# Attention operands stacked by selection matmuls, scores on 32-row tiles two heads at a time, and all experts kept in SBUF, in a two-block transformer kernel on one core

## What is computed

```python
x = x + tanh(g_xattn) * cross_attention(layernorm(x), ctx)       # one head of width 128, 512 keys of width 96
h = rmsnorm(layernorm(x)) * w1                                   # inner X = layernorm(x)
scores = q @ k.T / sqrt(8)                                       # 16 heads of width 8, 256 queries, 256 keys
X = layernorm(x) + softmax(scores) @ v @ wo
h2 = rmsnorm(X) * w2
moe = swiglu_shared(h2) + sum_e combine[:, e] * swiglu_e(h2)     # 8 experts, top 2, each 128 -> 256 -> 128
x = x + tanh(g_ffn) * (X + moe)
```

## Time and profile before

| what | value |
|---|---|
| median of 3 runs | 249.85 us (249.34 to 250.36) |
| the profiled execution, own time | 249.14 us |
| its span, first to last instruction | 247.4 us |
| mean granted TensorE clock | 0.922 |
| TensorE busy | 202.7 us (82%) |
| TensorE weight load busy | 161.2 us (65%) |
| VectorE busy | 152.5 us (62%) |
| ScalarE busy | 101.3 us (41%) |
| GpSimd busy | 58.8 us (24%) |

### The profile page before, as it was taken

How to read it: one execution, slowest core, us unless ns; L and a number is a source line. 1 busy time by engine, 2 the same in 40 slices (tenths; PEclk the granted TensorE clock), 3 DMA queues, 4 the chain that set the end, 5 groups by cost and what they waited for, 6 DMA issues and landing times.

```text
span 247.4 us, 3838 instructions
## 1 busy us (share of the span) xinstructions
PE 202.7 (82%) x1327; PEld 161.2 (65%) x1327; DVE 152.5 (62%) x393; ACT 101.3 (41%) x203; POOL 58.8 (24%) x77
## 2 busy tenths in 40 slices
PE   7699695659783798299888577899789999999994
PEld 5467464446572566167665455688668888888883
DVE  3779999647653175446687642478874654655653
ACT  8153265930162274246584565423231221221320
POOL 8566969310140020011011011003302332000000
PEclk9999998865679599869999999999979999999999
DMA  6900002535934023400000010000002230000002
GB/s 175 269 0 4 0 16 72 153 104 121 229 103 105 7 90 85 91 3 5 9 1 5 3 48 0 3 0 0 4 0 64 87 107 0 21 3 1 1 3 85
DMA packets 7124, 12.83 MB, mean 52 GB/s; under 512 B 992, under 2 KB 4576, under 8 KB 6592
## 3 DMA queue, kind: packets, MB, share of 16 engines
q1 hardware_dynamic: 7104, 12.58, 19.1%
HBM read 9.69 MB, written 2.62 MB: 50 GB/s over the span
## 4 chain that ended last, share of the span: by engine, by line
PE 48%; DVE 19%; DMA 12%; SPq 11%; issue 3%; ACT 3%; POOL 2%; DVEq 0%; ACTq 0%; POOLq 0%
PE bank L1066 12%; PE bank L1083 7%; PE bank L1085 6%; PE bank L1084 6%; DMA split_scratch<-split 5%; DMA q_st<-negmT 5%; PE bank L1052 5%; SPq L320 4%; SPq L323 4%; PE bank L1037 4%; PE bank L1026 3%; DVE mxs L822 2%; DVE xs L696 1%; DVE small L703 1%; DVE y L690 1%
## 5 line engine op out<-in xcount | busy, mean ns | idle before, releaser
L822 DVE TENSOR_REDUCE mxs<-bank 128x2 f32<-128x512 f32 x64 | 42.5, 689 | 27.9 <-PE bank L1026 27.4
L588 ACT ACTIVATE ep<-bank 128x512 f32<-128x512 f32 x64 | 37.5, 595 | 35.3 <-PE bank L1037 34.7
L1037 PE MATMUL bank<-q_st,k_st 128*128 128x256 f32 x128 | 28.8, 311 | 16.7 <-DMA q_st<-negmT 13.3
L1026 PE MATMUL bank<-k_st,q_st 128*128 128x256 f32 x128 | 34.3, 363 | 2.2 <-DVE mxs L822 1.1
L1066 PEld LDWEIGHTS bank<-down_s,vx 128*128 128x128 f32 x288 | 34.9, 193 | 1.8 <-issue 0.4
L1066 PE MATMUL bank<-down_s,vx 128*128 128x128 f32 x288 | 35.2, 276 | 0.0
L612 ACT ACTIVATE silu<-bank 128x512 f32<-128x512 f32 x28 | 16.6, 598 | 43.9 <-PE bank L1085 43.9
L1037 PEld LDWEIGHTS bank<-q_st,k_st 128*128 128x128 f32 x128 | 21.9, 210 | 18.5 <-DMA q_st<-negmT 13.9
L1083 PE MATMUL bank<-h2hi,whi 128*128 128x512 f32 x72 | 30.8, 428 | 2.7 <-ACT silu L612 2.7
L1026 PEld LDWEIGHTS bank<-k_st,q_st 128*128 128x128 f32 x128 | 23.5, 231 | 10.5 <-issue 4.5
L1085 PE MATMUL bank<-h2hi,wlo 128*128 128x512 f32 x72 | 29.1, 404 | 0.0
(11 more groups left out here) (139 smaller groups left out, 288.4 us busy)
## 6 DMA issues: line engine op xcount, KB each, us to landing
raw<-expert_w SPq DMA_DIRECT2D x9, 256.0 KB, 3.7
split_scratch<-split SPq DMA_DIRECT2D x16, 128.0 KB, 2.2
q_st<-split_scratch SPq DMA_DIRECT2D x16, 128.0 KB
k_st<-split_scratch SPq DMA_DIRECT2D x16, 128.0 KB
down_s<-expert_w SPq DMA_DIRECT2D x9, 128.0 KB, 2.7
ctxT<-ctx_T SPq DMA_DIRECT2D x1, 672.0 KB, 7.7
xs<-x_tiles SPq DMA_DIRECT2D x2, 256.0 KB, 4.2
out_dram<-x SPq DMA_DIRECT2D x2, 256.0 KB, 2.0
```

The source lines that it names most:

```text
L588: nc.scalar.activation(ep[:, n % NEP].rearrange("p t s -> p (t s)"), b_of(("exp", n))[:], ACT.Exp, scale=SCALE_H).then_inc(free(("exp", n) ...
L822: nc.vector.tensor_reduce(mxs[:, n // NH, :, n % NH], b_of(("max", n))[:].rearrange("p (t s) -> p t s", t=TB), AX_X, ALU.max).then_inc(fre ...
L1026: last = pe.matmul(b_of(("max", n))[:, j * L:(j + 1) * L], q_st[:, b % NSTACK, h // 2, j * P:(j + 1) * P], k_st[:, b % NSTACK, k_slot(h), ...
L1037: last = pe.matmul(b_of(("exp", n))[:, j * L:(j + 1) * L], k_st[:, b % NSTACK, k_slot(h), j * P:(j + 1) * P], q_st[:, b % NSTACK, h // 2, ...
```

## The change

Stacks: a 0/1 matrix `sel`, built on GpSimd from the identity, is multiplied with `split` on TensorE, 16 matmuls of 256 columns for each sequence, in a new step of x slot `SEL_AT` = 7 (plus 2 for each sequence). The results, `q4` and `k4`, hold four heads on four groups of 32 rows. They pass through four uses of the proj banks, the q ones copied by ScalarE, the k ones by VectorE. The scratch in DRAM, `stack`, the pads, the picks and the three stacks go; every sequence has its own `q4` and `k4`. Each score matmul contracts 32 rows at `tile_position` (r, 0).

Two heads at a time: on even slots both heads of a pair are done, the matmuls alternating between two row groups and two banks, and both banks of the pair must be free before the first of them. VectorE reduces both, ScalarE exponentiates both. `LAG` is 12.

Maxima: VectorE writes each head's maximum into a column of a zeroed 128-column tile, so that the transpose brings it to the row group of its head. The exp scores of a head begin with one matmul more, of 512 columns, with -1 in the row of the head (`pick`) and the maxima (`negm`) as the moving operand.

Experts: all nine are resident, weights are split as soon as they land and are never replaced. `NEARLY` is 8, so 24 thirds are early, from slot 62 on every second slot, from slot 76 on every slot. The x slots 8 to 13 are each followed by 3 a slots. C steps come one slot earlier.

```diff
-NSTACK = 3
-LAG = 13
+LAG = 12
...
-A_FROM = 10
-A_PER_X = 6
-M_FROM = 68
...
+A_FROM = 8
+A_PER_X = 3
+M_FROM = 62
 M_EVERY = 2
-T_FROM = 80
-T_EVERY = 2
-NEARLY = 4
+T_FROM = 76
+T_EVERY = 1
+NEARLY = 8
...
-NEP = 6
+SEL_AT = 7
+NEP = 8
 NRAW = 2
-NSPLIT = 4
...
+            b = sequence_at(i, SEL_AT)
+            if b is not None:
+                pair_uses["proj"] += [(name, b, part) for name in ("stq", "stk") for part in range(2)]
         if stage == "a":
-            if i < NHEADS:
-                pair_uses["turn"].append(("max", i))
-            if 0 <= i - LAG < NHEADS:
-                pair_uses["proj"].append(("exp", i - LAG))
+            if i < NHEADS and i % 2 == 0:
+                pair_uses["turn"] += [("max", i), ("max", i + 1)]
+            if 0 <= i - LAG < NHEADS and i % 2 == 0:
+                pair_uses["proj"] += [("exp", i - LAG), ("exp", i - LAG + 1)]
...
-        q_st = sb("q_st", [P, NSTACK, NG, L], F32R)
-        k_st = sb("k_st", [P, NSTACK, NH, L], F32R)
-        mxs = sb("mxs", [P, NB, TB, NH])
-        negmT = sb("negmT", [NH // 2, 2, L], F32R)
+        q4 = sb("q4", [P, NB, NQ, L], F32R)
+        k4 = sb("k4", [P, NB, NQ, L], F32R)
+        sel = sb("sel", [P, 2, 2, NQ, P], F32R)
+        pick = sb("pick", [P, 2, P], F32R)
+        pick_col = sb("pick_col", [P, 2])
+        mxs = sb("mxs", [P, 2, TB, P])
+        negm = sb("negm", [P, 2, L], F32R)
...
+        down_s = sb("down_s", [P, NEXP, FF])
+        whi, wlo = sb("whi", [D, NEXP, 2, FF], F32R), sb("wlo", [D, NEXP, 2, FF], F32R)
...
-        def stack(sp, b):
...
-                    sp.dma_start(scratch[b, qk, part].rearrange("p d g s -> (p d g) s"),
-                                 split[:, b % 2, part, qk, :].bitcast(F32)).then_inc(scratch_written[b], 16)
-            sp.wait_ge(scratch_written[b], 64)
...
-            for p in range(2):
-                for a in range(2):
-                    r = 32 * p + 16 * a
-                    q_src = scratch[b, 0, a, p].rearrange("d g s -> d (g s)").unsqueeze(1).broadcast_to([DH, 2, NG * L])
-                    sp.dma_start(q_st[r:r + 16, s].rearrange("r g s -> r (g s)").bitcast(F32),
-                                 q_src).then_inc(stacked[b], 16)
-                    k_src = scratch[b, 1, :, p].rearrange("c d g s -> d c (g s)")
-                    sp.dma_start(k_st[r:r + 16, s, p * NG:(p + 1) * NG].rearrange("r g s -> r (g s)").bitcast(F32),
-                                 k_src).then_inc(stacked[b], 16)
...
-        def place_m(sp, b, half):
...
-            src = negmT[:, i % 2, :].bitcast(F32).unsqueeze(1).broadcast_to([NH // 2, NG // 2, L])
-            sp.dma_start(q_st[r:r + 8, b % NSTACK, 4 * half:4 * half + 4, :].bitcast(F32), src).then_inc(m_placed[i], 16)
...
-            stack(sp, 0)
-            stack(sp, 1)
-            for e in range(NRAW, NSPLIT):
...
-            place_m(sp, 0, 0)
-            stack(sp, 2)
-            place_m(sp, 0, 1)
...
+            for e in range(NEXP):
                 load_expert(sp, e)
...
-            k_words = k_st[:, 0].bitcast(F32)
             pool.wait_ge(pool_step, done[0])
-            step(nc.gpsimd.memset(k_words[0:32, NG:], 0.0))
-            step(nc.gpsimd.memset(k_words[32:64, :NG], 0.0))
+            step(nc.gpsimd.memset(sel[:].rearrange("p a b g m -> p (a b g m)").bitcast(F32), 0.0))
...
+            def select_rows(qk, part):
+
+                rows = sel[:, qk, part].rearrange("p g (i r d) -> p (g i) r d", i=4, r=4)
+                rows = rows[:, :, 2 * part:2 * part + 2] if qk == 0 else rows[:, :, part::2]
+                heads = ident[:].rearrange("p (h d) -> p h d", d=DH).unsqueeze(2).broadcast_to([P, NH, 2, DH])
+                nc.gpsimd.tensor_copy(rows, heads).then_inc(sel_ready, 1)
...
-            def clear_pads(s):
-                words = k_st[:, s].bitcast(F32)
-                step(nc.gpsimd.memset(words[0:32, NG:], 0.0))
-                step(nc.gpsimd.memset(words[32:64, :NG], 0.0))
-                nc.gpsimd.memset(q_st[64:P, s].bitcast(F32), 0.0).then_inc(pads_ready, 1)
-                pool.wait_ge(pads_ready, s)
...
-            for b in range(NB - NSTACK):
-                is_read(pool, ("exp", NH * (b + 1) - 1))
-                pool.wait_ge(w_split, NSPLIT)
-                nc.gpsimd.memset(q_st[64:96, b % NSTACK].bitcast(F32), 0.0).then_inc(m_rows_zero, 1)
...
-                if i in (NT, NT + 1):
-                    copy_picks(i - NT + 1)
...
+                b = sequence_at(slot, SEL_AT)
+                if b is not None:
+                    for part in range(2):
+                        use = ("stq", b, part)
+                        is_full(act, use)
+                        nc.scalar.copy(q4[:, b, 2 * part:2 * part + 2, :].rearrange("p g s -> p (g s)"),
+                                       b_of(use)[:]).then_inc(free(use), 1)
...
-                n = slot - LAG
-                if 0 <= n < NHEADS:
...
+                first = slot - LAG
+                if 0 <= first < NHEADS and first % 2 == 0:
+                    for n in (first, first + 1):
+                        is_full(act, ("exp", n))
+                        if n >= NEP:
+                            is_full(act, ("pv", (n - NEP) // 4))
+                        nc.scalar.activation(ep[:, n % NEP].rearrange("p t s -> p (t s)"), b_of(("exp", n))[:],
+                                             ACT.Exp, scale=SCALE_H).then_inc(free(("exp", n)), 1)
...
+                b = sequence_at(slot, SEL_AT)
+                if b is not None:
+                    for part in range(2):
+                        use = ("stk", b, part)
+                        is_full(dve, use)
+                        nc.vector.tensor_copy(k4[:, b, 2 * part:2 * part + 2, :].rearrange("p g s -> p (g s)"),
+                                              b_of(use)[:]).then_inc(free(use), 1)
...
-                n = slot
-                if n < NHEADS:
...
+                if slot < NHEADS and slot % 2 == 0:
+                    for n in (slot, slot + 1):
+                        half, h = n // 8, n % NH
+                        if n == 0:
+                            dve.wait_ge(mxs_ready, 1)
+                        if n % 8 == 0 and half >= 2:
+                            is_full(dve, ("mT", (half - 2) // 2, half % 2))
+                        is_full(dve, ("max", n))
+                        c = 32 * (h % 4) + h // 4 % 2
+                        nc.vector.tensor_reduce(mxs[:, half % 2, :, c:c + 1],
+                                                b_of(("max", n))[:].rearrange("p (t s) -> p t s", t=TB),
+                                                AX_X, ALU.max).then_inc(free(("max", n)), 1)
...
+                b = sequence_at(slot, SEL_AT)
+                if b is not None:
+                    if b == 0:
+                        pe.wait_ge(sel_ready, 4)
+                    pe.wait_ge(hi_ready, b + 1)
+                    is_read(pe, ("qk2", b))
+                    for qk, name in ((0, "stq"), (1, "stk")):
+                        for part in range(2):
+                            use = (name, b, part)
+                            may_fill(pe, use)
+                            for g in range(2):
+                                for hl in range(2):
+                                    last = pe.matmul(b_of(use)[:, g * L:(g + 1) * L], sel[:, qk, hl, 2 * part + g, :],
+                                                     split[:, b % 2, hl, qk, :], start=(hl == 0), stop=(hl == 1))
+                            last.then_inc(full(use), 1)
...
-                        last = pe.transpose(b_of(use)[0:NH // 2, j * P:(j + 1) * P],
-                                            mxs[:, b, j, 8 * half:8 * half + 8], ident[:])
+                        last = pe.transpose(b_of(use)[:, j * P:(j + 1) * P], mxs[:, half, j, :], ident[:])
...
-                if n < NHEADS:
+                if slot < NHEADS and slot % 2 == 0:
+                    b, h = slot // NH, slot % NH
+                    if h == 0:
+                        for part in range(2):
+                            written(("stq", b, part))
+                            written(("stk", b, part))
+                    may_fill(pe, ("max", slot))
+                    may_fill(pe, ("max", slot + 1))
+                    for j in range(TB):
+                        for o in range(2):
+                            r, use = 32 * ((h + o) % 4), ("max", slot + o)
+                            last = pe.matmul(b_of(use)[:, j * L:(j + 1) * L],
+                                             q4[r:r + 32, b, h // 4, j * P:(j + 1) * P], k4[r:r + 32, b, h // 4, :],
+                                             start=True, stop=True, tile_position=(r, 0))
+                            if j == TB - 1:
+                                last.then_inc(full(use), 1)
+                n = slot - LAG
+                if 0 <= n < NHEADS and n % 2 == 0:
                     b, h = n // NH, n % NH
-                    if h == 0:
```

(36 more changed lines are left out.)

127 lines of the change are left out of this document (36 added, 91 removed).

## The result

The changed kernel takes 261.9 us, the median of 4 runs (261.22 to 264.06), beside 249.59 us for the kernel before on the same chip: 1.051 times, interval [1.0434, 1.0586]. It is 5% slower where 3% faster was forecast, and outside the range of 230 to 257 us. Ratios here are taken from a kernel's undisturbed runs, medians from all of its runs, so for a kernel that scatters the two can differ. The third rival has come true, and it covers more slots than it was priced for.

A forecast was written before the change was run, and what follows sets the result against it. Stack transfers and VectorE were taken to bound the first half, TensorE the second. Last maximum at 128.7 us plus 111.0 gave a span of 239.7, forecast as 242 us against 249.85, 3% faster; range 230 to 257 us.

The forecast's parts named there:

- third rival: In the a slots the clock falls, four heads take 7 us against 4.3; 258 us at half the slots; chance 0.15.
- A: Up to the first maximum: transfers and pad memsets go, so it starts 10.8 us earlier, at 43.5 us.
- B: Heads 0 to 17 between x slots: reductions, x work, refills and selection waits take 23.4 us, ending at 66.9 us.
- C: Heads 18 to 63: 61.8 us, with a refill exposed in every pair and four heads in 4.3 us.
- D: From the last maximum to the end: 111 us, from 108.5 plus 5.0 less 2.5; bounds 106 and 117.
- the term of the selection: In part B, k copies wait twice behind the selection's bank uses and ScalarE's copies, 0.9 us each: 1.8 us.
- the full clock: In the a slots the clock was expected full, as from 87 to 99 us before, despite 0.97 us waits.
- at the lower level for a quarter of 45 to 130 us: Sign that the forecast is wrong: TensorE's clock at its lower level for that share of the stretch.
- the first rival: Row tiles overlap in full, loads too, so pairs with v take 1.9 us: 233 us in all; chance 0.22.
- Early thirds move work and remove none: In part D a third costs the same before or after the last maximum; filling idle time gains 2 us.
- The rule on tiling modes: Skill says changing tiling mode drains the array, adding 6.4 us to part C; the forecast charged 0.1 us instead.
- The rule on row tiling: Skill reports 3.07 times for four row tiles of 512 columns; by it, fully overlapping row tiles would be the forecast.

The follow-up runs named there:

- experiment 2: Two kernels against the changed one: pairs kept, score matmuls over all 128 rows, 255.53 us; 32 rows kept, single heads for pairs, 276.71 to 295.35 us.
- experiment 7: Changed kernel with single heads and full-row matmuls on zero-padded copies of k: 239.5 us; second kernel, selection alternating and a slots later: 238.76 us.
- experiments 2 and 6: The second of these: changed kernel with single heads for pairs and score matmuls over all 128 rows (scores of four heads summed): 235.47 us.
- experiment 3: Changed kernel with 12 early thirds instead of 24, one every second slot: 270.45 and 272.48 us.
- experiment 4: Changed kernel, three unread full-array matmuls behind pairs without products with v: 253.88 us; also with selection alternating 252.99, plus another filler 252.81; with 12 thirds 262.86.
- experiment 5: Changed kernel with single heads, LAG 13, alternating row groups: with two unread full-array matmuls every even slot 246.98 to 259.91 us, with one 255.75 to 269.74 us.

## Why the prediction was wrong, by its steps

| part | predicted | measured | difference |
|---|---|---|---|
| A, first maximum at | 43.5 | 41.52 | -2.0 |
| B, to the end of head 17 | 23.4 | 30.6 | +7.2 |
| C, to the end of the last maximum | 61.8 | 81.1 | +19.3 |
| D, to the end | 111.0 | 109.1 | -1.9 |
| span | 239.7 | 262.3 | +22.6 |

**A was right** and a little cautious. The norms of sequence 0 got the gain that was charged.

**B: the term of the selection was mis-sized.** The k copies waited 3.00 and 3.68 us for it, where 0.9 each was charged: 4.9 of the 7.2 us. The lower clock is the smaller part of it. It was down for both selections, and 16 matmuls that take 2.4 us at full clock (8 in 1.20) took 3.81. But with full rows in pairs (experiment 2) the second selection ran at full clock, and the k copy behind it still waited 3.21 us; in the first kernel of experiment 7, at full clock and without pairs, both copies waited 2.04 us.

```profile
70.34 1.29 DVE L676 CAST k<-bank 128x512 fp32r<-128x512 f32 x2 [3.21 <-PE bank L921]
```

So 0.9 was too little at any clock. A further 1.8 of the 7.2 us are two norm passes of a sequence that ran beside weight splits on GpSimd (L383, 48.78 and 50.69 us), an effect that part A charged and part B left out: 1.34 and 1.51 us, where 0.59 and 0.48 are the times alone (39.53 and 40.16 us). The last half us stays open.

```profile
49.35 1.34 DVE L621 TENSOR_SCALAR y<-x,mv,small 128x128 f32<-128x128 f32 x2
50.72 1.51 DVE L627 TENSOR_SCALAR xs<-y,small 128x128 f32<-128x128 f32 x2
```

**C: the step that failed is the full clock.** The prediction took it from 87 to 99 us of the earlier trace rows, where the kernel before holds it over 0.97 us of waiting in four heads. But those scores contract 128 rows, so the row could not speak for 32. The prediction named the mechanism and its place and gave it 0.15; the condition "at the lower level for a quarter of 45 to 130 us" came true (mean 0.63 over these 85 us, so about three quarters of them). Its price was a little high: 7 us for four heads, measured 6.5 and 5.9. The excess of 1.6 to 2.2 us over 11.5 groups of four is 18 to 25 us, and 19.3 are missing. Half of the slots at that level, for 258 us, was its example; in truth nearly all of part C was (76.8 to about 151 us of 72.14 to 153.23). It named two reasons together, a TensorE that waits and matmuls on 32 rows, and experiments 2 and 6 show that the second is enough: busy 29.05 of 30 us, clock 0.50.

**C, at full clock, was charged too much.** Four heads were to take 4.3 us and took 3.9 with three fillers in them. Loads for different row groups don't keep the 0.11 us of the earlier trace rows: they start two at a time, two in 0.18 us and all four in 0.30. So the first rival's mechanism is real for the two row groups of a pair, only hidden under the clock; it had put four heads at 3.9 us. That the pair exposes a refill was right (0.65 and 0.66 us idle, as forecast), and on full rows it was dear: 20 us by experiments 2 and 6, part of it by the clock. Before, one bank was filled while the other was read; the step from 3.67 to 3.9 us for four heads shows only a part of this, where the rest falls was not measured. Nor was the price of the pair for row tiles, whose refill is shorter than that of the full rows that gave the 20 us.

**D was right as a sum, but not in its reason.** The 108.5 us it starts from begin where the last maximum starts (138.89 us), while part C runs to its end: 0.7 us stand in the sum twice, and D should have been 110.3. "Early thirds move work and remove none" is refuted by experiment 3: twelve fewer cost 9.6 us, where 2 us were counted for all of it. The sum took a third to cost the same wherever it stands; in experiment 3 most of what this stretch gained in length can be the clock. What used this gain up in the changed kernel was not taken apart; the clock is at 0.86 from 153 to 160 us and 0.97 over all of D. At full rows and single heads the same stretch takes 102.9 us, at a clock of 1.00.

**The rule on tiling modes.** By the Trainium skill (TensorEngine Tiling, Key Properties) a drain would have added 6.4 us to part C. The full-clock pairs of experiment 4 leave no room for it: 3.9 us for four heads with turns in them, less than the 4.3 that charged 0.1 for them. A price of about 0.1 us a turn can be seen: two full-array fillers between tiles took 0.66 us (84.03 to 84.69 in experiment 5), and a full-array matmul of 512 columns in a row of such takes 0.23 to 0.24 (210.26 to 210.50 and on to 210.73 us before), which leaves 0.18 us for two turns.

**The rule on row tiling.** The Trainium skill (TensorE: Matmul & The Clock Gate, Part 3) recommends four row tiles for a short contraction, by a factor of 3.07. The trace agrees that row tiles overlap: at full clock four matmuls on two row groups pass in the time that two take on the full array. But no row of this case shows a list of such matmuls that keeps that clock without full-array work in between. For the kernel's time the measured 41 us decide.

## What to carry to other kernels

Row tiling cuts the time of a matmul, and can take the clock from all that stands beside it. Look at the granted clock of the stretch, not at TensorE's busy share: 29 of 30 us busy was no protection. Before a list is moved from full to 32-row contractions, try it with the operand padded by zeros to full rows; here that, together with single heads for pairs, was 22 us faster than the row tiles. And a step that wants both halves of a double buffer at once gives the buffer up: price the refill for every step, and the clock that the added waits can cost.
